# A graph attention layer on one core: the turned adjacency stored in the order of its loads, 8 KB of a partition in one piece

## The reference

```python
h = jnp.maximum(_layernorm(x, axis=-1), 0.0)          # x: 4096 x 128
x = x + _L0_gnn_ref(h, adj, W, b_W, a_vec, b_a)

def _L0_gnn_ref(node_features, adjacency_matrix, W, b_W, a_vec, b_a):
    h = node_features @ W.T + b_W
    a1, a2 = (a_vec[:D_OUT], a_vec[D_OUT:])
    e = (h @ a1)[:, None] + (h @ a2)[None, :] + b_a[0]
    e = jnp.where(e > 0, e, 0.2 * e)
    scores = jnp.where(adjacency_matrix > 0, e, jnp.float32(NEG_INF))
    attention = jax.nn.softmax(scores, axis=1)
    return attention @ h
```

## Time and profile before

| | |
|---|---|
| median of 3 runs | 208.16 us (207.99 to 208.33) |
| profiled execution | 207.64 us, of which the span of the core 206.1 us |
| PE busy | 198.3 us (96% of the span) |
| DVE busy | 183.7 us (89%) |
| ACT busy | 142.3 us (69%) |
| DMA | 75.66 MB in 24160 packets, mean 367 GB/s |

### The profile page before, as it was taken

How to read it: one execution, slowest core, us unless ns; L and a number is a source line. 1 busy time by engine, 2 the same in 40 slices (tenths; PEclk the granted TensorE clock), 3 DMA queues, 4 the chain that set the end, 5 groups by cost and what they waited for, 6 DMA issues and landing times.

```text
span 206.1 us, 7172 instructions
## 1 busy us (share of the span) xinstructions
PE 198.3 (96%) x3183; PEld 192.1 (93%) x3183; DVE 183.7 (89%) x271; ACT 142.3 (69%) x129; POOL 43.5 (21%) x60
## 2 busy tenths in 40 slices
PE   7969999999999999999999999999999999999794
PEld 7648878999999999999999999999999999999694
DVE  4779889999999699987999999979999998979954
ACT  2679777798771777689777775797577767897000
POOL 1002479599995010420000000000000000000000
PEclk9999999999999999999999999999999999999999
DMA  5999999999999999999999999999999999992312
GB/s 180 364 411 405 400 410 406 406 409 406 408 432 398 406 410 409 405 409 409 405 409 411 400 387 417 409 408 407 409 406 408 359 413 414 408 405 118 99 47 64
DMA packets 24160, 75.66 MB, mean 367 GB/s; under 512 B 1600, under 2 KB 5952, under 8 KB 24000
## 3 DMA queue, kind: packets, MB, share of 16 engines
q1 hardware_dynamic: 23984, 75.06, 92.7%
q10 hardware_dynamic: 144, 0.13, 0.3%
HBM read 73.08 MB, written 2.11 MB: 365 GB/s over the span
## 4 chain that ended last, share of the span: by engine, by line
DMA 63%; ACT 14%; PE 6%; issue 6%; DVE 5%; SPq 4%; DVEq 0%
DMA adj_sb<-in_adj_t 63%; ACT mask L379 10%; DVE w L459 4%; ACT xT L394 3%; SPq L268 2%; PE ps L834 2%; PE ps L836 2%; PE ps L840 2%; SPq L273 2%; PE ps L808 1%; SPq L284 1%; DVE xT L497 1%; ACT H L342 1%; PE ps L798 0%; ACT hT L337 0%
## 5 line engine op out<-in xcount | busy, mean ns | idle before, releaser
L834 PE MATMUL ps<-V,w 128*128 128x129 f16 x1024 | 177.3, 219 | 1.2 <-DVE w L459 1.2
L836 PE MATMUL ps<-V,w 128*128 128x129 f16 x1024 | 177.3, 223 | 0.0
L840 PE MATMUL ps<-V,w 128*128 128x129 f16 x1024 | 177.3, 218 | 0.0
L379 ACT ACTIVATE mask<-adj_sb 128x2048 bf16<-128x2048 int32 x63 | 119.9, 1915 | 39.1 <-DMA adj_sb<-in_adj_t 38.9
L459 DVE SCALAR_TENSOR_TENSOR w<-g_row,pairs,mask 128x1024 f32<-128x1024 f32 x96 | 117.7, 1282 | 9.5 <-ACT mask L379 8.5
L834 PEld LDWEIGHTS ps<-V,w 128*128 128x128 f16 x1024 | 99.2, 97 | 3.0 <-DVE w L459 1.6
L840 PEld LDWEIGHTS ps<-V,w 128*128 128x128 f16 x1024 | 102.0, 100 | 0.0
L836 PEld LDWEIGHTS ps<-V,w 128*128 128x128 f16 x1024 | 99.8, 97 | 1.0 <-issue 1.0
L459 DVE SCALAR_TENSOR_TENSOR w<-ps,pairs,mask 128x1024 f32<-128x1024 f32 x31 | 37.6, 1271 | 1.3 <-ACT mask L379 1.3
L788 POOL PARTITION_ALL_REDUCE bad<-bad x1 | 0.4, 380 | 114.6 <-DVE bad L532 114.6
L746 POOL TENSOR_TENSOR x_sb<-x_sb,b_row 128x512 f32<-128x512 f32 x8 | 10.0, 1304 | 0.0
(11 more groups left out here) (93 smaller groups left out, 62.4 us busy)
## 6 DMA issues: line engine op xcount, KB each, us to landing
adj_sb<-in_adj_t SPq DMA_DIRECT2D x64, 1024.0 KB, 11.2
xT<-in_x_t SPq DMA_DIRECT2D x8, 256.0 KB, 7.9
x_sb<-in_x_p SPq DMA_DIRECT2D x3, 512.0 KB, 11.3
g_row<-g_dram SPq DMA_DIRECT2D x1, 1536.0 KB, 10.6
out<-xT SPq DMA_DIRECT2D x3, 512.0 KB, 11.5
x_sb<-in_x_p SPq DMA_DIRECT2D x2, 256.0 KB, 4.5
out<-xT SPq DMA_DIRECT2D x1, 192.0 KB, 2.1
out<-xT SPq DMA_DIRECT2D x3, 64.0 KB, 1.5
```

What stands on the lines that cost most here:

```text
L379: nc.scalar.activation(mask[:, m % MASKS, :], adj_sb[:, m % HELD, :], ACT.Relu, scale=CONNECTED).then_inc(mask_ready, 1)
L834: nc.tensor.matmul(sums[:, bank, a, :], w16[:, m % SLOTS, col:col + P, 1], V[:, jt, 0:NF], start=(jt == 0 and a == 0), stop=False, skip_gr ...
L836: nc.tensor.matmul(sums[:, bank, a, :], w16[:, m % SLOTS, col:col + P, 1], V[:, jt, NF:2 * NF], start=False, stop=False, skip_group_check= ...
L840: last = nc.tensor.matmul(sums[:, bank, a, :], w16[:, m % SLOTS, col:col + P, 0], V[:, jt, 0:NF], start=False, stop=(jt == NT - 1), skip_g ...
```

## The change

The host already turned the adjacency. It now also lays it out in 64 blocks of 128 x 2048 words, block m being what load m fetches: for each partition the 1024 words of the first tile of the pair, and behind them those of the second. The load becomes one piece of 8 KB a partition in place of two pieces of 4 KB that lay 2 MB apart. The words that arrive, the place in `adj_sb` where they arrive, the number and order of the loads and their waits are as before; no other instruction differs.

```diff
+_GROUP = 8
...
-    GI = 8
+    GI = _GROUP
...
-        adjt_v = adj_t.rearrange("(g p) n -> p g n", p=P)
...
                 def load_adj(m):
-                    group, at = divmod(m, PAIRS)
...
-                    sp.dma_start(adj_sb[:, m % HELD, :].rearrange("p (a n) -> p a n", a=2),
-                                 adjt_v[:, 2 * at:2 * at + 2, group * GC:(group + 1) * GC]
-                                 ).then_inc(adj_loaded[m % HELD], 16)
+                    sp.dma_start(adj_sb[:, m % HELD, :], adj_t[m, :, :]).then_inc(adj_loaded[m % HELD], 16)
...
-    arrays["in_adj_t"] = np.ascontiguousarray(np.asarray(inputs["adj"]).T)
+    adj = np.asarray(inputs["adj"])
+    pairs = adj.shape[0] // (2 * P)
+    arrays["in_adj_t"] = np.ascontiguousarray(
+        adj.T.reshape(pairs, 2, P, -1, _GROUP * P).transpose(3, 0, 2, 1, 4).reshape(-1, P, 2 * _GROUP * P))
```

## The result

The changed kernel takes 205.43 us (median of 6 executions, 204.78 to 206.81), the kernel before 208.07 us beside it (median of 6, 207.47 to 211.45). The ratio is 0.987, with a 95% interval of 0.983 to 0.992: faster, as forecast, but by 2.6 us and not by 1.8. Two later comparisons, with more executions of the kernel before, gave 0.983.

A forecast was written before the change was run, and what follows sets the result against it. PE was taken to bound the long middle, with transfers costing time only at front and tail. 0.26 + 1.53 = 1.8 us off the median of 208.16 gave 206.4 us, range 205.7 to 208.2.

The forecast's parts named there:

- the front: Up to block 4 on PE: loads 0 to 3 land sooner, so block 4 begins 0.26 us sooner.
- the 0.52 us: Added to go from the profiled execution, 207.64 us, to the median of the runs shown, 208.16.
- The packet: Each adjacency load, as 8 KB packets in place of 4 KB, saves 0.06 to 0.09 us; 0.065 taken.
- the middle: Transfers run 3.8 us ahead by block 58; PE is not faster, and the time goes into DVE's lead.
- the tail: Last blocks: both PE holes, waits for DVE's weights of block 63, close and give 1.53 us.
- Rival A: Adjacency transfers: memory, not packets, sets 408 GB/s, so nothing moves; 208.2 us, chance 0.10.
- rival C: Adjacency loads as solid megabytes become 1% slower, 404 GB/s; 209.8 us, chance 0.07.
- of the 0.42 us hole 0.195 goes: Front: of PE's 0.42 us wait for the relu behind mask 3, 0.195 us was to go.
- All of it moves by the 0.26 of the front alike: Tail: DVE's and PE's last blocks all come 0.26 us sooner, on top of the 1.53 us from closed holes.
- my own case: Whole kernel: both holes at the end close and block 4 begins sooner; 206.0 to 206.9 us, chance 0.65.
- Rival B: End of the kernel: holes close by half, 0.8 us, and the start gives 0.1; 207.3 us, chance 0.10.
- Rival D: Start of the kernel gives up to 0.8 us, block 0 much earlier by cheaper issues or emptier queues; 205.8 us, chance 0.08.

The follow-up runs named there:

- solid4k: The changed kernel with every load still one solid megabyte, but fetched in pieces of 4 KB: 208.87 us, ratio 1.001 to the kernel before.
- after_again: The changed kernel once more, unedited, for a second profile: 205.21 us, ratio 0.983 to the kernel before.
- after_third: The changed kernel again, unedited, as the control of later runs: 205.26 us.
- last24_8k: The changed kernel with only loads 40 to 63 in pieces of 8 KB, the others in 4 KB: 206.80 us, ratio 0.994 to the kernel before.
- before_less1mb: The kernel before, 4 KB pieces, with loads 36 and 37 fetching only their first tile, 1 MB less: 206.32 us, ratio 0.990 to the kernel before.
- rest_8k: The changed kernel with loads 0 to 3 in pieces of 4 KB and loads 4 to 63 in 8 KB: 205.55 us, ratio 0.984 to the kernel before.
- before_again: The kernel before once more, unedited, for a second profile: 207.6 us.
- first4_8k: The changed kernel with only loads 0 to 3 in pieces of 8 KB, the other 60 in 4 KB: 208.50 us, ratio 1.000 to the kernel before.
- early_8k: The changed kernel with only loads 4 to 17 in pieces of 8 KB, the other 50 in 4 KB: 206.88 us, ratio 0.993 to the kernel before.

## Why the forecast was right in its direction and wrong in its size

Two steps of the prediction failed, and both were sizes: the 0.26 us of the front, where the profile had 0.77 to give, and the 0.52 us that were added to go from the profiled execution to the median, as if both kernels had the same spread. The packet, the middle and the tail came as forecast.

**The packet.** Right. 0.065 us a load was taken, 0.062 measured; a long row is not cut; the packets were forecast near 15970 and are 15968. Rival A (memory sets the rate) falls with 418 GB/s, rival C (a solid megabyte is slower) with `solid4k`.

**The middle.** Right: PE's step was unchanged and the saved time went into lead, which paid at the tail alone. The lead was smaller than forecast in half of the profiles. At block 58 the transfers were 2.4 us (`after_again`) and 2.7 us (`after_third`) ahead of the profile of before, and 3.9 and 3.8 in the other two, where 3.8 was forecast. All were enough, or within 0.4 us of it.

**The tail.** The mechanism was right, in the place and order forecast: both holes closed, no wait for the mask of block 59, DVE waiting for PE instead. That the time of the transfers does it is shown by the rule of mask 58 + 26.52, which holds with pieces of either length; `last24_8k` fits it too. `before_less1mb` fits it in its profile, but its median missed its expectation by 1.0 us.

**The front.** This is the first term that was mis-sized: "of the 0.42 us hole 0.195 goes", and 0.26 us in all. I had read the hole from the modelled idle time. The starts show more. Between the matmuls of blocks 0 to 3, PE's breaks before were 1.91, 2.01 and 2.49 us; after, they are 1.91, 1.86 and 1.87. That is 0.77 us, and PE had it all to give. Mask 3, which waits for load 3, began at 27.00 in the profile before and at 26.00 in that after, 1.00 and not 0.26 sooner. With 0.77 + 1.53 = 2.30 the last matmul would be forecast at 202.95 - 2.30 = 200.65 us. It stands at 200.53 to 200.74 in the three profiles with an early rise of the clock.

How much of that 0.77 is the change's is not shown. Over all profiles mask 3 began between 26.0 and 27.5 in the thirteen with these loads in 4 KB pieces (median 26.45), and between 25.7 and 26.3 in the five with 8 KB (26.00). The profile of before was in the later half of its own spread. In `rest_8k`, with loads 0 to 3 as before, the breaks were 1.91, 1.86 and 1.93 all the same, and its 205.55 us lie 0.3 above `after_again`, within the spread of each. The third break was 1.86 in three of the seven profiles of the kernel before and 2.94 in `before_again`. So the sum was made against a hole that comes and goes.

**From one execution to the median.** The second half of the miss: "All of it moves by the 0.26 of the front alike", and 1.8 us taken off the median as off the profile. The two kernels hang on different things. The kernel before ends by its transfers, whatever its front does (`first4_8k`, `before_again`); so the front's gain is one only once the tail is free. Its spread is upwards, to 208.9 with the clock up, which in the profiles (up to 208.45) goes with later transfers, and to 209 and 210 with a fall of the clock in a third of the executions. Without the executions at 0.992 the medians of the kernel before are 207.87, 207.61 and 207.93 in place of 208.35, 207.91 and 208.26, so that fall is 0.3 to 0.5 us of the gain. The changed kernel ends by PE's start and has none of these. From fastest to fastest (207.47 and 204.78) the gain is 2.7 us, from median to median 2.6 in the first comparison and 3.0 or 3.1 in two later ones. The profiled execution that the sum was made against was near the fast end. My "median is 0.52 higher" was a constant, and it should have been a spread that the change takes away. A slip beside it: the low end of my own case, 206.0, does not follow from "0.42 + 1.53 at the most", which gives 206.2; that changes nothing here.

**Rival B** (half of the tail) did not come. **Rival D** (more from the front) named a place for more, but its cause, a much earlier block 0, isn't the one: load 0 landed at 12.1 to 13.1 us with 4 KB pieces in thirteen profiles and at 12.1 to 13.2 with 8 KB in five. The rows show no difference that could be told from the spread.

**Left open.** That the clock falls in the executions of 209 to 210 us in the kernel before is on record for 23 of 24; that it falls in the holes of the tail, and why it does so in some executions with these holes and not in others, is not shown, since no profile of the kernel before caught one. Nor is shown why load 58 lands up to 1.3 us sooner or later from one execution of the kernel before to the next (175.9 to 177.2), where the lead of loads 4 to 17 passes load 17, or what makes three of the twelve executions of `before_less1mb` longer than 207 us.

## What to carry to other kernels

Where a stream of transfers runs without a pause and another engine is slower by a little, look for the place where the slower engine speeds up (here the last four blocks, which PE takes in 1.04 us steps): there the stream's lead is spent, and a saving of 2% in each load is worth more than its share of the middle says. Before one side of such a race is made faster, write down what the end of each side hangs on; a gain in front of the side that waits is worth nothing until the other is out of the way. And take more than one profile of the kernel before where its times spread by 1% or more: one execution gives one sample of each hole. Where a row names an engine that had long been done with the thing waited for, as with mask 17 above, look for the transfer that landed at that moment before you build a theory on the name.

## What the runs showed of the hardware

- A packet of 8 KB takes 309 ns at its most frequent (315 in the mean) on one DMA engine, two of 4 KB 2 x 159 (2 x 164 in the mean), one of 12 KB 465 (460 in the changed kernel), one of 2 KB 84. From 84, 159 and 309 that is some 9 ns a packet beside 75 ns for every 2 KB. It is the same whether or not the block is solid in memory: 159 ns at its most frequent in `solid4k` too. These are the durations of single packets in the traces.
- The 16 engines drift apart. Block 50 landed on the first engine 4.6 us before the last one in the profile of before, and a load counts only when the last has landed. Each of the 25 packets that fetch instructions takes about 1.06 us of one engine (0.8% of 16 x 206 us on the page's queue q8, over 25). The landing times make jumps of about that size, where load 24 spread over 2.7 us and load 25 over 3.5; that the fetches cause them is not shown.
- TensorE's clock reached 2.4 GHz at 4.3 to 10.9 us, with the engine busy from 1.22 us on. In the changed kernel that is a difference of 1.0 to 1.2 us in the whole time (206.40 against 205.25 to 205.45).
- With holes of 0.7 to 1.3 us between groups of matmuls at the tail, the clock fell to 1.2 GHz for 3.4 us in one profile (`early_8k`) and stayed at 2.4 GHz in another with the same holes (`first4_8k`).
